# Delta attention in half chunks: state scalings between copies of hops, sums without zero products, four gates between state updates

## The reference

```
q, k, v = silu(conv(x @ Wq)), silu(conv(x @ Wk)), silu(conv(x @ Wv))   # 16 heads of 128
a = sigmoid(x @ Wa + ba); beta = sigmoid(x @ Wb + bb)
for t in time:                       # S: 128 x 128 for each of batch x head = 64 lanes
    err = S @ k_t - v_t
    S   = a_t * S - (beta_t * err) k_t^T
    o_t = S @ q_t
out = (layernorm(o) * sigmoid(x @ Wg)) @ Wo
```

## Time and profile before

| | us |
|---|---|
| median of 3 runs | 2721.2 (2713.15 to 2727.33) |
| the profiled execution | 2719.86 |
| its span, first to last instruction | 2717.9 |

### The profile page before, as it was taken

How to read it: one execution, slowest core, us unless ns; L and a number is a source line. 1 busy time by engine, 2 the same in 40 slices (tenths; PEclk the granted TensorE clock), 3 DMA queues, 4 the chain that set the end, 5 groups by cost and what they waited for, 6 DMA issues and landing times. The chain is left out here.

```text
span 2717.9 us, 45341 instructions
## 1 busy us (share of the span) xinstructions
PE 2118.7 (78%) x16952; PEld 1637.6 (60%) x16952; DVE 1517.7 (56%) x3266; ACT 1176.9 (43%) x2893; POOL 1031.6 (38%) x966
## 2 busy tenths in 40 slices
PE   8597449978988968676796767977689776778798
PEld 5364126656566856565686656766567665546686
DVE  2223732256564347677586776866767667346532
ACT  3112311136464427553564535645356453326433
POOL 0322022210004534767137672375723756100254
PEclk9698769989898989877797668977689776879899
DMA  8422022210007014221222212221122311120330
GB/s 283 125 24 53 0 70 42 24 38 3 21 2 230 0 19 126 60 67 55 78 86 65 67 56 86 78 75 57 55 86 79 83 48 55 39 57 2 103 128 15
DMA packets 138317, 179.47 MB, mean 66 GB/s; under 512 B 62048, under 2 KB 114544, under 8 KB 132992
## 3 DMA queue, kind: packets, MB, share of 16 engines
q1 hardware_dynamic: 129952, 166.46, 20.0%
q0 software_dynamic: 8160, 10.26, 2.4%
HBM read 154.52 MB, written 22.17 MB: 65 GB/s over the span
## 5 line engine op out<-in xcount | busy, mean ns | idle before, releaser
L2655 DVE SCALAR_TENSOR_TENSOR XT<-M_delta,CW_delta,XT 128x256 f32<-128x256 f32 x576 | 249.8, 494 | 79.2 <-ACT M_delta L2460 49.7
L2148 PE MATMUL PS<-XP_delta,X 128*128 128x268 f32 (+1 forms) x1024 | 241.4, 388 | 15.9 <-DMA X<-in_L_attn_b_heads 15.8
L2148 PEld LDWEIGHTS PS<-XP_delta,X 128*128 128x128 f32 x1024 | 192.7, 189 | 67.4 <-DMA X<-in_L_attn_b_heads 20.1
L1541 PE MATMUL PS<-XP_rffn,UW_rffn 128*128 128x512 f32 x816 | 194.9, 396 | 5.0 <-POOL UW_rffn L1495 4.6
L1541 PEld LDWEIGHTS PS<-XP_rffn,UW_rffn 128*128 128x128 f32 x816 | 156.0, 192 | 38.8 <-issue 5.9
L1273 ACT ACTIVATE PR_attn<-PS,NM_attn 128x256 f32<-128x256 f32 (+1 forms) x384 | 130.7, 448 | 103.5 <-DVE NM_attn L1343 103.5
L1495 POOL TENSOR_TENSOR UW_rffn<-W_rffn,UW_rffn 128x512 fp32r<-128x512 f32 x34 | 44.2, 1300 | 301.4 <-ACT UW_rffn L1602 301.4
L2585 ACT ACTIVATE S_delta<-S_delta,AO_delta 128x128 f32<-128x128 f32 x512 | 157.6, 396 | 0.0
L561 POOL DMA_INDIRECT sums<-XS_moe,token_moe x46 | 71.7, 1559 | 221.5 <-ACT XS_moe L661 207.0
L1663 DVE TENSOR_TENSOR SU_rffn<-PS,CB_rffn 128x512 f32<-128x512 f32 x68 | 47.0, 691 | 179.6 <-PE PS L1541 156.6
L1504 POOL TENSOR_TENSOR HP_rffn<-HF_rffn,HP_rffn 128x512 fp32r<-128x512 f32 x68 | 92.4, 1378 | 116.0 <-ACT HP_rffn L1625 116.0
...
## 6 DMA issues: line engine op xcount, KB each, us to landing
...
```

The lines of the kernel that those rows point to most:

```text
L1541: last = nc.tensor.matmul(PS[:, 4 + 2 * n + q, :], UW[qw][:, r, (q * KD + k) * P:(q * KD + k + 1) * P], XP[qx][:, k, n * NB:(n + 1) * NB], ...
L2148: last = nc.tensor.matmul(PS[:, 1 + i, 0:B * (WIN - halo)], WH[:, r, i, k, :], XP[:, k, :, n * BT + halo:n * BT + WIN], start=(k == 0), st ...
L2655: nc.vector.scalar_tensor_tensor(TMP[:, r, i], RAW[:, r, i, :, tau:tau + BT], CW[:, i, h, tau:tau + 1], TMP[:, r, i], ALU.mult, ALU.add).t ...
```

## The change

1. The tile ZB, its memset on POOL and the four zero products ahead of the hops of jj = 1 and 2 are gone. The first matmul of the first hop starts each bank, the others add.
2. The scalings of the state are cut by another table, 14, 14, 20 and 16 lanes for the four chunks. For jj of 1 and 2 eight lanes follow L2609's copy and six follow each hop's copy but the last; none stand between `answer` and the next chunk's copies (for jj = 0 with gates, nine stay with the gates).
3. `answer` comes ahead of the gates on ACT.
4. Gates 12 to 15 leave the last chunk. They stand in `heads_and_norm`, two after the first state update and two after the second on PE, after `answer` on ACT. Centre, variance and spread move behind them: variance and spread now come after the fourth update, and DVE's `shift` after the fourth sum.
5. On ACT the last two of the four groups of key rows come after the chunk's `answer` (o = 0, jj = 1) or after the last 16 scalings (o = 1, jj = 3).

```diff
--- before.py
+++ after.py
@@ -1725,7 +1725,6 @@
     BETAH = sb("BETAH", [P, 2, T // C])
     SAME = sb("SAME", [P, B])
     SAMEH = sb("SAMEH", [P, 2 * B])
-    ZB = sb("ZB", [P, 4 * QU], BF16)
     MB = sb("MB", [P, NI, 4, B])
     AO = sb("AO", [P, BH])
     PJ = sb("PJ", [P, BH])
@@ -1802,7 +1801,6 @@
             nc.gpsimd.memset(DD[:], 1.0)
             nc.gpsimd.memset(DC[:], 1.0)
             nc.gpsimd.memset(DR[:], 1.0)
-            nc.gpsimd.memset(ZB[:], 0.0)
             nc.gpsimd.memset(S[:], 0.0)
 
         @block.tensor
@@ -1880,7 +1878,7 @@
     sc_out = [s.sem(f"sc_out{j}") for j in range(NC)]
     by_b = lambda t: t.rearrange("p (h b) w -> p b h w", b=B)
     rests = lambda o, jj: (NI - 1) * o + jj
-    beside = lambda o, jj: (range(NR) if jj == (NI - 1 if o else 1) else (), range(4 * jj, 4 * jj + 4) if o else ())
+    beside = lambda o, jj: (range(NR) if jj == (NI - 1 if o else 1) else (), range(4 * jj, 4 * jj + 4) if o and jj < NI - 1 else ())
     WH4, NH4 = TR[:, 1, 0:BH * HC], TR[:, 1, BH * HC:]
     flat_df = DF[:].rearrange("p n t -> p (n t)")
     MH = flat_df[:, 0:4 * B * NI].rearrange("p (j g l) -> p j g l", j=NI, g=2)
@@ -2267,8 +2265,8 @@
                 for i in range(4):
                     for k in range(4):
                         rows, at = slice(OC * k, OC * (k + 1)), slice(i * QU, (i + 1) * QU)
-                        last = nc.tensor.matmul(PS[:, 1 + k, at], NEW[rows, i], GN[rows, BLOCKS.index((s, jj + 1)), at], start=jj == 0,
-                                                stop=jj == 0 or (s == jj and i == 3))
+                        last = nc.tensor.matmul(PS[:, 1 + k, at], NEW[rows, i], GN[rows, BLOCKS.index((s, jj + 1)), at],
+                                                start=s == 0 and i == 0, stop=s == jj and i == 3)
                 if s == jj:
                     last.then_inc(rest_mm, 1)
 
@@ -2348,13 +2346,20 @@
                 if n:
                     if n < NBLK:
                         update(n - 1, NO - 1, 0)
+                    pe.wait_ge(wt_d, NR * NO * n)
+                    gate(n - 1, H - 4)
+                    gate(n - 1, H - 3)
+                    if n < NBLK:
+                        update(n - 1, NO - 1, 1)
+                    gate(n - 1, H - 2)
+                    gate(n - 1, H - 1)
+                    if n < NBLK:
+                        update(n - 1, NO - 1, 2)
+                    pe.wait_ge(gate_d, H * n)
                     centre(n - 1, 0)
                     if n < NBLK:
-                        update(n - 1, NO - 1, 1)
+                        update(n - 1, NO - 1, 3)
                     variance(n - 1, 0)
-                    if n < NBLK:
-                        update(n - 1, NO - 1, 2)
-                        update(n - 1, NO - 1, 3)
                     spread(n - 1, 0)
                 for k in range(1, H // 2 + 1):
                     if n and k < NW:
@@ -2401,8 +2406,6 @@
                             pe.wait_ge(cn_d, z["cn_d"] + 2 * o + 2)
                         elif jj < NI - 1:
                             pe.wait_ge(res_d, z["res_d"] + ci + 1)
-                            for k in range(4):
-                                nc.tensor.matmul(PS[:, 1 + k, 0:4 * QU], ZB[:, 0:P], ZB[:], start=True, stop=False)
                             for x in range(jj):
                                 hop(n, o, jj, x)
                         if jj + 1 < NI:
@@ -2418,7 +2421,7 @@
                             pe.wait_ge(kr_d, z["kr_d"] + NR * (o + 1))
                         for h in gates:
                             gate(n, h)
-                        if o:
+                        if gates:
                             pe.wait_ge(gate_d, z["gate_d"] + 4 * jj + 4)
                     pe.wait_ge(w_d, z["w_d"] + NI * (o + 1))
                     pe.wait_ge(wdec_d, z["wdec_d"] + rests(o, NI - 1))
@@ -2492,6 +2495,8 @@
 
                 if n:
                     answer(n - 1, NC - 1)
+                    for h in range(H - 4, H):
+                        gate(n - 1, h)
                     square(n - 1, 0)
                 for k in range(1, H // 2 + 1):
                     if n and k < NW:
@@ -2590,7 +2595,7 @@
                 act.wait_ge(nw_mm, base_of(n)["nw_mm"] + HOPS * o + hop_no(jj, s) + 1)
                 nc.scalar.copy(TR[:, 2], PS[:, 6, :]).then_inc(nw_d, 1)
 
-            cuts = [0, 14, 22, 22, 34, 40, 48, BH, BH]
+            cuts = [0, 14, 28, 48, BH]
             for n in range(NBLK):
                 z = base_of(n)
                 heads_and_norm(n)
@@ -2610,24 +2615,36 @@
                         if jj == 0:
                             cross_products(n, o)
                             act.wait_ge(ds_d, z["ds_d"] + o + 1)
+                        lane, last = cuts[jj:jj + 2]
+                        if 0 < jj < NI - 1:
+                            decay_state(lane, lane + 8)
+                            lane += 8
                         if jj < NI - 1:
                             for x in range(jj + 1):
                                 hop(n, o, jj, x)
+                                if x < jj:
+                                    decay_state(lane, lane + 6)
+                                    lane += 6
                         if jj == NI - 2:
                             act.wait_ge(wdec_d, z["wdec_d"] + rests(o, jj))
                             for x in range(jj):
                                 natural(x)
-                        for r in rows:
+                        for r in rows[:2]:
                             key_rows(n, o, r)
-                        at, then = cuts[2 * jj:2 * jj + 2]
-                        for h in gates:
-                            gate(n, h)
-                            decay_state(at, min(at + 3, then))
-                            at = min(at + 3, then)
-                        decay_state(at, then)
-                        if jj + 1 < NI:
+                        if gates:
+                            then = max(lane, last - 9)
+                            decay_state(lane, then)
                             answer(n, ci)
-                            decay_state(then, cuts[2 * jj + 2])
+                            for h in gates:
+                                gate(n, h)
+                                lane, then = then, min(then + 3, last)
+                                decay_state(lane, then)
+                        else:
+                            decay_state(lane, last)
+                            if jj + 1 < NI:
+                                answer(n, ci)
+                        for r in rows[2:]:
+                            key_rows(n, o, r)
                     for r in range(NR):
                         turn(n, o, r)
                     if o + 1 < NO:
@@ -2810,11 +2827,9 @@
                     if n < NBLK:
                         dve.wait_ge(sdec_d, n * NO)
                         add_update(n - 1, NO - 1, 0)
-                        add_update(n - 1, NO - 1, 1)
+                        for r in range(1, NR):
+                            add_update(n - 1, NO - 1, r)
                     shift(n - 1, 0)
-                    if n < NBLK:
-                        add_update(n - 1, NO - 1, 2)
-                        add_update(n - 1, NO - 1, 3)
                 for k in range(1, H // 2 + 1):
                     if n:
                         gated(n - 1, k - 1)
```

## The result

| | before | after |
|---|---|---|
| median of 6 runs, us | 2718.9 (2713.2 to 2727.3) | 2659.2 (2648.1 to 2663.8) |
| ratio, 95% interval | | 0.977 (0.9744 to 0.9797) |
| profiled execution, us | 2719.86 | 2658.91 |
| span | 2717.9 | 2657.0 |

The change is faster by 2.3%. The profiled execution after ends 60.95 us sooner, and lies at the median of its runs. The forecast was 2655, the range 2640 to 2676.

What follows compares the result with a forecast made beforehand. Three DVE waits in delta attention, behind ACT's fixed order, bound the kernel. Carries 69.6 plus turn 1.5, less transitions 4.5 and last block 1, gave 65.6 off 2719.86: 2654.3, forecast 2655, range 2640 to 2676.

Steps and rivals of the forecast that it cites:

- (a): First outer chunk, jj = 2: scalings out of the gap, carry at 1505.5 instead of 1508.09; 2.5 us a block.
- (b): Second outer chunk, jj = 1: PE turns after the gates, carry at 1593.1 instead of 1596.71; 3.6 us a block.
- (c): Second outer chunk, jj = 2: carry at 1613.2 instead of 1616.98; 3.8 us a block.
- (d): First outer chunk, jj = 3: zeros' 1.18 off the hop chain, 1.1 from POOL's shifted work; 2.3 us a block.
- (e): Second outer chunk, jj = 3: gates sooner, no scalings between; carry at 1637.1 instead of 1642.27; 5.2 us a block.
- I take 1.18 for each set: Zero products ahead of the hops: 2.65 us to the hop's products against 1.47 without them, so 1.18 a set.
- Turn term: Block's end, last carry to update 0: 13.6 us instead of 14.13; gain 0.5, 1.5 over three blocks.
- Between the updates: Update 0 to the next head: 18.0 us against 17.24, more at low clock; loss 1.5 for each of three transitions.
- Cold gates: Rival: at the block's end PE's clock is low, update rounds last 5.7 instead of 3.7 us: 2671; chance 0.15.
- POOL becomes the bound: Rival: in delta attention POOL and DVE hold each other up, 8 times 1.5 us: 2667; chance 0.12.
- The scalings fall on the hops: Rival: on ACT the moved scalings hold the hop copies, 82 us: 2737; chance 0.02, in part only 0.02.
- The clock helps: Rival: gates keep PE warm through the transitions and the last layernorm: about 2644; chance 0.06.

Runs made afterwards that it cites:

- the part alone: Only the zero products removed from the kernel before, the first hop's matmul opening each bank: 2701.6 us, ratio 0.9937.
- the early shift alone: Changed kernel with the first variance ahead of the fourth update and DVE's shift ahead of the fourth sum: 2642.4 us, ratio 0.9722.

## Why the prediction was right, and where not

**What bounds, and the main cause: right.** The three waits of the earlier trace rows were the place, and ACT's fixed order the reason: the scalings alone won 45.4 and their old place took 37.6 back. The separate numbers of the text came so: the wait for the answer gone (forecast under 3), idle time ahead of a hop copy 1.45 (1.4), update rounds 3.67 apart (3.7), POOL's product at 1.2 (no more than 1.2). The carry's wait is 22.4, a little over the 15 to 20 written; the wait for the last hop is 9 times and 14.8 in all, near 8 times 1.97, but only the four of the first outer chunks are alike.

**The five terms (a) to (e), each for one block.** (a) 2.5, measured 2.5 (82.7 to 72.8 for four). (b) 3.6, measured 4.0. (c) 3.8, measured 3.0. (d) 2.3, measured 1.9. (e) 5.2, measured 4.6. The gaps of jj = 1 in the first outer chunk and of jj = 0 in the second together gained 0.15, where nothing was forecast. Sum 16.1 where 17.4 was forecast. These are averages of four blocks; in the second outer chunks single gaps differ by up to 1.9 between blocks. The estimate under (a) and (c), 2.8 from the handover to the carry, was 3.17 where it can be read (above), 0.4 short: it counted the turn and the copy, and left out that PE's product also waits for DVE's queries' side.

**"I take 1.18 for each set" was mis-sized.** A set of zeros costs 0.77. The step compared a stretch of PE at one clock with one at another: the hop without zeros at 1477.02 has its turn in 0.66, at the upper level, the hop with zeros at 1509.16 stood where the granted clock was 0.50, the lower level (1.2 GHz). The window of the first, in the kernel before:

```profile
1476.00:1478.00 2.00, 0.66 (x4) 0.42 (x4) 1.93 (x6) 1.20 (x3) 1.84 (x3) 1.00 0.00 0
```

A hop without zeros at the lower level is in the changed kernel's PE, with its window:

```profile
1493.04 1.12 PE L2261 MATMUL PS<-ident,WNS_delta 128*128 128x128 f32 x4 [1.19 <-DVE TR_delta L2729]
1494.92 1.98 PE L2268 MATMUL PS<-GN_delta,TR_delta 32*128 32x64 f32 x32 [0.77 <-ACT TR_delta L2596]
...
1491.00:1498.00 7.00, 4.99 (x56) 3.91 (x54) 5.92 (x19) 3.92 (x14) 6.45 (x8) 0.50 0.00 0
```

1.88 from turn to product, and 2.65 less 1.88 is 0.77. With 0.41 less in (d), that term would have been 1.9, as measured. A second thing the text lacked is that in the kernel before the zeros cost twice in a first outer chunk, once more through ACT; this changes no sum of the whole change, since (a) to (c) were worked out from where the carry can come, but it is one reason why the part alone gave 19 and not 6.

**(d) and POOL.** L2738 beside POOL's product took 2.80 before. In the changed kernel L2755, the same instruction, takes 1.70 at 1509.76. POOL in the changed kernel there:

```profile
1508.27 2.91 POOL L2099 TENSOR_TENSOR M_delta<-M_delta,DD_delta 128x1280 f32<-128x1280 f32 x1
1511.26 2.96 POOL L2062 TENSOR_TENSOR DD_delta<-DD_delta,A_delta 128x128 f32<-128x128 f32 x3
```

L2755 ends at 1511.46, 0.28 after the POOL instruction that was running (1511.18), and the carry follows at 1511.49. With no POOL instruction beside it, at 4 of its 32 places, L2755 takes 0.41; at the other 28 it ends 0.27 to 0.28 after the POOL instruction that ran when it started. So it waited for the running instruction to end, and for no longer: 1.10 less than before, which with the zeros' 0.77 is the 1.9 measured for (d). Elsewhere POOL's earlier work collides more: for jj = 1 of the second outer chunk L2755 takes 1.75, where L2738 took 0.92. There the carry comes only 1.39 after it ended, so nothing was lost. The Trainium skill, "SBUF — State Buffer", section "SBUF: two separate sides", describes this: VectorE, with both inputs in SBUF as in L2755, and GpSimd take turns at a port pair, a whole instruction at a time. By it (d) was to stay near 2.3 in place of 2.9; the trace agrees that VectorE waits for the instruction that runs.

**Turn term, "Gain 0.5": mis-sized, measured 2.1 for each of three transitions.** The composition was right (13.6 forecast after the carry, 12.9 to 13.1 measured), but block 1's 14.13 was taken for all three, and before it was 15.56 and 15.65 in the others. Reading one block where three count makes 3.0 of the 4.9 us that came on top; the other 1.9 is that update 0 came 0.6 sooner than composed.

**Between the updates, "a loss of 1.5 for each": mis-sized, measured 2.4 each**, 7.2 in three, inside the bounds of 2.4 and 9. The low clock behind the fourth sum, priced at 2 us and then taken only in part, was the case in all three: 2.07 and 1.91 for spread and centre, where I had 1 and 1, so 3.57 from spread to head and not 2. In block 1 update 0 took 2.09 and not 1.17 too, another 0.9. The first head, at 5.01, 4.12 and 4.08 against 3.76, lies behind this stretch, and H to C0 shows no loss from it beyond 0.6. That the order and not the gates was the cause is shown by the early shift alone: 16.8 came back, with the gates where the change put them.

**Last block: loss of 1 forecast, 0.6 gained**, inside its bounds of 4 lost and 2 won, and no more than chance. With the zeros back, which don't touch this stretch, it took 65.5 and not 68.9, so an execution varies here by more than the change does.

**Ahead of delta attention 3.3 us were lost that no term had**, 2.4 at the first head already. The first head begins at 1028.6 before, at 1031.0 after, and between 1028.3 and 1036.6 in the variants, though the code ahead of it is the same but for ZB's memset: that is how one execution differs from another, and so no sign of the change. What it comes from stays open.

**The rivals.** *Cold gates* did not come: two gates take 1.99 to 2.21, and updates 1.17 but for one of 2.09 in block 1. The Trainium skill, "TensorE: Matmul & The Clock Gate", section "Part 4: PE-mode transpose", let one expect that a turn alone does not warm PE. The trace is divided on it, and mostly against it: behind 5.57 of idle time and the turn, update 0 took 2.09 in block 1; behind 6.03 and the turn (1302.01, 3.60) it took 1.17 in block 0 (1305.53), and the same in block 2. In block 0 the granted clock was 0.50 from 1302 to 1305 and 1.00 from 1305.5 on, with only idle time and transposes ahead of it. *POOL becomes the bound:* no, 1.2 each as before. *The scalings fall on the hops:* not with six; with twelve they do, for 0.2 a hop: only what exceeds the idle time counts, and the rival's 0.30 for every lane would have been far too much. *The clock helps:* through the updates only; what it gave there the later `shift` took back. The top of the range, 2676, was written as the sum of the first two rivals; their own prices, 16 and 12, give 2683. The measured time is not touched by it.

The total came this near partly by luck, because errors went both ways. Against a forecast gain of 65.6 the chunks gave 5.1 less, the turn 4.9 more, the updates 2.7 less, the last block 1.6 more, the stretches ahead of C0 3.9 less; that makes 60.4.
